# Feature attention of a perceiver block on one core: both sides held transposed, scores on 32 rows, the norm in the exponent, the division on 128x128

## What is computed

```python
def favorplus_features(x, proj):
    xw = jnp.einsum('bhtd,hmd->bhtm', x, proj)
    xw = xw - jnp.max(xw, axis=-1, keepdims=True)
    x_norm_sq = jnp.sum(x * x, axis=-1, keepdims=True)
    return jnp.exp(xw) * jnp.exp(-0.5 * x_norm_sq) + EPS
...
Q = heads(Wq) / math.sqrt(dk)
K = heads(Wk) / math.sqrt(dk)
V = heads(Wv)
phiQ = favorplus_features(Q, proj) * inv_sqrt_m
phiK = favorplus_features(K, proj) * inv_sqrt_m
KV = jnp.einsum('bhtm,bhtd->bhmd', phiK, V)
Ksum = jnp.sum(phiK, axis=2)
num = jnp.einsum('bhtm,bhmd->bhtd', phiQ, KV)
den = jnp.einsum('bhtm,bhm->bht', phiQ, Ksum)[..., None] + EPS
out_heads = num / den
return jnp.einsum('btd,ed->bte', merged, Wo) + bo
```

## Time and profile before

| | us |
|---|---|
| median of 3 runs | 4464.28 |
| runs | 4464.1 to 4465.34 |
| the profiled execution, its own time | 4462.0 |
| its span, first to last instruction | 4460.2 |
| TensorE busy, of the span | 4198.4 (94%) |
| VectorE busy | 2030.8 (46%) |
| ScalarE busy | 1409.1 (32%) |
| GpSimd busy | 159.6 (4%) |
| mean granted clock of TensorE | 0.970 |

### The profile page before, as it was taken

One profiled execution on the slowest core, in us unless ns is written; L12 is line 12 of the kernel. 1 busy time (PEld: TensorE's weight loads), 2 busy tenths in 40 slices (PEclk: granted clock), 3 DMA queues, 4 the chain that ended last, 5 costly groups with the idle time before them and its releaser, 6 DMA issues. The chain is left out here.

```text
span 4460.2 us, 60595 instructions
## 1 busy us (share of the span) xinstructions
PE 4198.4 (94%) x24096; PEld 2764.1 (62%) x24096; DVE 2030.8 (46%) x4307; ACT 1409.1 (32%) x3812; POOL 159.6 (4%) x167
## 2 busy tenths in 40 slices
PE   8999999999999998998799989999999999986885
PEld 4767676767677666665464435666666666763443
DVE  3333333333333333255443334666666666564445
ACT  3222222222222321344231003444444444332232
POOL 0000000000000000022110000000000000000000
PEclk9999999999999999999899999999999999997887
DMA  4010101010101001201304002111011011001000
GB/s 161 29 48 29 54 22 57 25 52 29 57 20 57 29 19 52 96 20 39 99 20 137 0 27 77 44 51 42 25 52 42 24 53 48 1 1 43 0 0 26
DMA packets 86512, 190.47 MB, mean 43 GB/s; under 512 B 7792, under 2 KB 16624, under 8 KB 84464
## 3 DMA queue, kind: packets, MB, share of 16 engines
q1 hardware_dynamic: 73072, 138.60, 9.3%
q0 software_dynamic: 13184, 48.24, 3.4%
HBM read 170.04 MB, written 16.78 MB: 42 GB/s over the span
## 5 line engine op out<-in xcount | busy, mean ns | idle before, releaser
L470 PE MATMUL swishmax_attended<-swishmax_weights_t,swishmax_context 128*128 128x256 f32 x4096 | 905.1, 379 | 0.0
L470 PEld LDWEIGHTS swishmax_attended<-swishmax_weights_t,swishmax_context 128*128 128x128 f32 x4096 | 768.4, 190 | 99.2
L1393 PE MATMUL context_bank<-context_context_t,context_wk 128*128 128x512 f32 x1024 | 475.6, 607 | 17.6 <-DMA context_context_t<-in_context_t_dram 17.6
L485 PE MATMUL swishmax_bank<-swishmax_context_t,swishmax_w_key 128*128 128x512 f32 x1024 | 476.1, 608 | 15.1 <-DMA swishmax_context_t<-in_context_t_dram 15.1
L1262 ACT ACTIVATE context_exps<-context_score,context_neg_max 128x512 f32<-128x512 f32 x512 | 345.1, 686 | 379.6 <-DVE context_neg_max L1296 379.6
L352 ACT ACTIVATE swishmax_xes<-swishmax_score,swishmax_neg_max 128x512 f32<-128x512 f32 x256 | 164.4, 687 | 839.2 <-DVE swishmax_neg_max L389 839.2
L1393 PEld LDWEIGHTS context_bank<-context_context_t,context_wk 128*128 128x128 f32 x1024 | 185.0, 190 | 298.8 <-issue 292.0
L1296 DVE TENSOR_REDUCE context_neg_max<-context_score 128x1 f32<-128x512 f32 x512 | 317.5, 682 | 113.4 <-PE context_score L1361 113.3
L485 PEld LDWEIGHTS swishmax_bank<-swishmax_context_t,swishmax_w_key 128*128 128x128 f32 x1024 | 185.2, 190 | 296.6 <-issue 295.1
L389 DVE TENSOR_REDUCE swishmax_neg_max<-swishmax_score 128x1 f32<-128x512 f32 x256 | 164.7, 685 | 426.8 <-PE swishmax_score L456 426.8
L1408 PEld LDWEIGHTS context_bank<-whole_ident,context_exps 128*128 128x128 f32 x2048 | 229.1, 141 | 119.2 <-issue 69.7
(11 more groups left out here) (341 smaller groups left out, 4838.1 us busy)
## 6 DMA issues: line engine op xcount, KB each, us to landing
swishmax_context_t<-in_context_t_dram SPq DMA_DIRECT2D x32, 1024.0 KB, 5.3
swishmax_context<-in_context_dram POOLq DMA_DIRECT2D x32, 1024.0 KB, 5.8
context_context_t<-in_context_t_dram SPq DMA_DIRECT2D x32, 1024.0 KB, 5.4
ahead_context_t<-in_context_t_dram SPq DMA_DIRECT2D x14, 1024.0 KB, 6.5
ahead_values<-ahead_staged SPq DMA_DIRECT2D x14, 1024.0 KB, 8.4
context_values<-ahead_values POOLq DMA_DIRECT2D x56, 256.0 KB, 3.5
experts_w<-in_L_ffn_W_dram SPq DMA_DIRECT2D x16, 512.0 KB, 8.5
whole_x<-in_x_dram SPq DMA_DIRECT2D x8, 256.0 KB, 8.1
```

What stands on the lines that cost most here:

```text
L470: last = nc.tensor.matmul(attended[m // 2][:, m % 2, :], context[:, c, k, m * P:(m + 1) * P], weights_t[:, n % 2, k].rearrange("p r q -> p ...
L485: last = nc.tensor.matmul(bank_t[:], w_key[:, k, g * P:(g + 1) * P], context_t[:, c, k, :], start=k == 0, stop=k == DC - 1)
L1393: last = nc.tensor.matmul(bank_t[:], w["k"][:, k, g * P:(g + 1) * P], context_t[:, c, k, :], start=k == 0, stop=k == DC - 1)
```

## The change

`kernel_attention` is written anew; its inputs, and the other parts, stay, but for two counters in them that become one (`first = link = Chain(dve, chain)`).

- The sides are made transposed at once: the weights are the stationary operand and the normed tokens the moving one, 16 matmuls of 128 columns each; `side`, side_t and their transposes go.
- Scores are 16 matmuls of 32 rows by 128 columns a side, each head on its own quarter of the array's rows; score bank r holds head r of each group. `proj` is no longer block-diagonal: four loads, no zeros.
- The norm: ScalarE squares the transposed side, TensorE sums it per head with a matrix of ones of four columns (norms, 8 matmuls for both sides), VectorE writes -norm/2 + log(1/sqrt(m)), adds it to the negated maximum, and the exponential takes that as its bias. ScalarE writes the features; EPS is added by VectorE on the query side and by GpSimd on the key side, 128x512 at a time.
- `values` has 64 columns a head: 32 values, and 32 of which column h//4 is one. From the sums, den (one 128x128 for all heads, 16 matmuls on 32 columns of the array each, accumulated) and num (likewise, 128x512) come out transposed. VectorE adds EPS to the 128x128 and inverts it; a matmul with `select` spreads each row over its head's 32 rows; VectorE multiplies. heads_t needs no transposes.
- The loop over pairs is gone. In slot t the engines make the front of sequence t, the scores of t-1 and the back of t-2, by three lists, one for each engine, over ten slots. One ring of four banks serves both emptying engines.
- The output bias is added to x ahead of time, by GpSimd. The first sequence no longer waits for `loaded`.

The diff, cut to its core, the removed lines left out (they stand above):

```diff
...
+        hidden_t = s.sb("hidden_t", [P, 2, DC, P])
+        side_t = s.sb("side_t", [P, 2, 2, NG, P])
+        squares_t = s.sb("squares_t", [P, 2, 2, NG, P])
+        half_norm = s.sb("half_norm", [P, 2, 2, HG, NG])
+        values = s.sb("values", [P, 2, H, 2 * HD])
+        neg_max, exp_bias = s.sb("neg_max", [P, 2, 2, HG, NG]), s.sb("exp_bias", [P, 2, 2, HG, NG])
+        features = s.sb("features", [P, 2, 2, HG, NG, M])
+        features_t = s.sb("features_t", [P, 2, HG, NG, P])
+        sums = s.sb("sums", [P, 2, H, 2 * HD])
+        select = s.sb("select", [P, NG, P])
+        number = s.sb("number", [P, NG, P])
+        inverse = s.sb("inverse", [P, P])
+        heads_t = s.sb("heads_t", [P, NG, P])
...
+        bank = [s.ps(f"bank{n}", [P, CH]) for n in range(4)]
+        score = [s.ps(f"score{r}", [P, CH]) for r in range(HG)]
...
+        def pe_slot(t):
+            p, c, o = t < B, 0 <= t - 1 < B, 0 <= t - 2
+            out = [("score", t - 1, KEY)] * c + [("features_t", t - 2, r) for r in range(HG)] * o + [("hidden", t, 0)] * p
+            out += [("den", t - 2, 0)] * o + [("side", t, QUERY)] * p + [("num", t - 2, 0)] * o
+            out += [("score", t - 1, QUERY)] * c + [("side", t, KEY)] * p + [("spread", t - 2, 0)] * o + [("value", t, 0)] * p
+            out += [("norms", t, QUERY), ("norms", t, KEY)] * p + [("output", t - 2, 0)] * o
+            return out + [("sums", t - 1, 0), ("sums", t - 1, 1)] * c
...
+        def dve_slot(t):
+            p, c, o = t < B, 0 <= t - 1 < B, 0 <= t - 2
+            out = [("max", t - 1, KEY, 0)] * c + [("features_t", t - 2, 1), ("features_t", t - 2, 3)] * o
+            out += [("max", t - 1, KEY, r) for r in (1, 2, 3)] * c + [("den", t - 2, 0)] * o
+            out += [("side", t, QUERY)] * p + [("norm", t + 1)] * (t + 1 < B)
+            out += [("max", t - 1, QUERY, r) for r in range(HG)] * c + [("side", t, KEY)] * p
+            out += [("heads", t - 2)] * o + [("norms", t, QUERY), ("norms", t, KEY)] * p
+            out += [("feature", t - 1, QUERY, r) for r in (0, 1)] * c + [("output", t - 2, 0)] * o
+            return out + [("feature", t - 1, QUERY, r) for r in (2, 3)] * c + [("sums", t - 1, 0)] * c
...
+        pe_steps = [x for t in range(B + 2) for x in pe_slot(t)]
+        act_steps = [x for t in range(B + 2) for x in act_slot(t)]
+        dve_steps = [("norm", 0)] + [x for t in range(B + 2) for x in dve_slot(t)]
+        BY_SCALAR = {("value", 0), ("features_t", 0), ("features_t", 2), ("hidden", 0), ("num", 0), ("sums", 1)}
+        ring = SharedRing(bank, [t for t in pe_steps if t[0] != "score"], {"a": full_a, "d": full_d}, {"a": out_a, "d": out_d},
+                          lambda t: "a" if (t[0], t[2]) in BY_SCALAR else "d")
...
+                pool.wait_ge(loaded, 16 * LOADS)
+                for b in range(B):
+                    pool.wait_ge(normed_x, b + 1)
+                    nc.gpsimd.tensor_tensor(x_sb[:, b, :], x_sb[:, b, :], bias_o[:], ALU.add).then_inc(biased_x, 1)
+                    for r in range(HG):
+                        pool.wait_ge(exped, set_no(b, KEY) * HG + r + 1)
+                        nc.gpsimd.tensor_scalar(features[:, b % 2, KEY, r], features[:, b % 2, KEY, r], EPS * INV_SQRT_M, None,
+                                                ALU.add).then_inc(key_featured, 1)
...
+                    if what == "exp":
+                        r = t[3]
+                        act.wait_ge(biased, set_no(b, n) * HG + r + 1)
+                        for g in range(NG):
+                            last = nc.scalar.activation(features[:, e, n, r, g, :], score[r][:, g * M:(g + 1) * M], ACT.Exp,
+                                                        bias=exp_bias[:, e, n, r, g:g + 1])
+                        last.then_inc(exped, 1)
+                    elif what == "square":
+                        act.wait_ge(out_d, ring.count(("side", b, n)))
+                        nc.scalar.activation(squares_t[:, e, n], side_t[:, e, n], ACT.Square).then_inc(squared, 1)
...
+                    if what == "max":
+                        q, r = t[2], t[3]
+                        if r == 0:
+                            dve.wait_ge(out_d, ring.count(("norms", b, q)))
+                        dve.wait_ge(scored, set_no(b, q) * HG + r + 1)
+                        link(nc.vector.tensor_reduce(neg_max[:, e, q, r, :], score[r][:].rearrange("p (g m) -> p g m", m=M),
+                                                     AX.X, ALU.max, negate=True))
+                        nc.vector.tensor_tensor(exp_bias[:, e, q, r, :], neg_max[:, e, q, r, :], half_norm[:, e, q, r, :],
+                                                ALU.add).then_inc(biased, 1)
...
+                    if what == "heads":
+                        t = ("spread", b, 0)
+                        dve.wait_ge(out_a, ring.count(("num", b, 0)))
+                        dve.wait_ge(full_d, ring.count(t))
+                        nc.vector.tensor_tensor(heads_t[:], number[:], ring.bank(t)[:].rearrange("p (g q) -> p g q", q=P), ALU.mult).then_inc(out_d, 1)
+                        continue
+                    n = t[2]
+                    dve.wait_ge(full_d, ring.count(t))
+                    bank_t = ring.bank(t)
+                    if what == "den":
+                        nc.vector.tensor_scalar(inverse[:], bank_t[:, 0:P], EPS, None, ALU.add).then_inc(out_d, 1)
+                        dve.wait_ge(out_d, ring.count(t))
+                        nc.vector.reciprocal(inverse[:], inverse[:]).then_inc(inverted, 1)
...
+                    if what == "score":
+                        k = set_no(b, n)
+                        evicted(("side", b, n))
+                        pe.wait_ge(loaded, 16 * LOADS)
+                        if k:
+                            pe.wait_ge(exped, k * HG)
+                        for g in range(NG):
+                            for r in range(HG):
+                                rows = slice(r * HD, (r + 1) * HD)
+                                last = nc.tensor.matmul(score[r][:, g * M:(g + 1) * M], side_t[rows, e, n, g, :], proj[rows, g, :],
+                                                        start=True, stop=True)
+                                if g == NG - 1:
+                                    last.then_inc(scored, 1)
+                        continue
...
+                    elif what == "side":
+                        evicted(("hidden", b, 0))
+                        name = "qk"[n]
...
+                                last = nc.tensor.matmul(bank_t[:, g * P:(g + 1) * P], w[name][:, c, g * P:(g + 1) * P], hidden_t[:, e, c, :],
+                                                        start=c == 0, stop=c == DC - 1)
...
+                    elif what == "norms":
+                        pe.wait_ge(squared, 2 * b + n + 1)
+                        pe.wait_ge(grouped, 1 + HG)
+                        for g in range(NG):
+                            last = nc.tensor.matmul(bank_t[:, g * HG:(g + 1) * HG], squares_t[:, e, n, g, :], group[:], start=True, stop=True)
...
+                        for g in range(NG):
+                            for r in range(HG):
+                                last = nc.tensor.matmul(bank_t[r * HD:(r + 1) * HD, 0:P], sums[:, e, HG * g + r, HD:2 * HD],
+                                                        features_t[:, e, r, g, :], start=g == 0, stop=g == NG - 1)
+                    elif what == "num":
+                        for g in range(NG):
+                            for r in range(HG):
+                                last = nc.tensor.matmul(bank_t[r * HD:(r + 1) * HD, g * P:(g + 1) * P], sums[:, e, HG * g + r, 0:HD],
+                                                        features_t[:, e, r, g, :], start=True, stop=True)
+                    elif what == "spread":
+                        pe.wait_ge(inverted, b + 1)
+                        pe.wait_ge(selected, NG)
+                        for g in range(NG):
+                            last = nc.tensor.matmul(bank_t[:, g * P:(g + 1) * P], select[:, g, :], inverse[:], start=True, stop=True)
...
```

346 lines of the change are left out of this document (132 added, 214 removed).

## The result

The changed kernel takes 4335.51 us (median of four runs, 4330.9 to 4336.68), the kernel before 4464.19 in the same comparison: a ratio of 0.9711, 95% interval 0.9694 to 0.9727. It is 129 us faster, as forecast (4335.5). The profiled execution took 4336.0 us, 2.0 more than its span.

What follows compares the result with a forecast made beforehand. The stage was taken as bound by TensorE's own work, its unoverlapped waits and the clock falling for both; slot work, waits and clock summed to 244.1 us, 128.8 off the end, so 4335.5 us, range 4320 to 4368.

Steps and rivals of the forecast that it cites:

- The sum: Whole attention stage, all ten slots: 244.1 us from 4023.91, its end 128.8 us earlier, median 4335.5 us.
- TensorE's work, 26.6 and 0.3 for tiling: One full slot: 26.6 us of TensorE matmuls, plus some 0.3 lost between whole-array and 32-row or 32-column ones.
- The wait at den: In a full slot, TensorE idle 0.95 us ahead of den until ScalarE empties the third features_t bank.
- an excursion: In a slot, switching from whole-array to 32-row or 32-column matmuls and back: four a slot, some 0.3 us together.
- eight changes at the 0.2 of the prediction: Tiling-mode switches in a slot, by the skill's drain rule: no more than 0.2 us each, total 13 us later.
- Slots 0 to 2 and the tail: Stage's ends: slot 0 18.4 us, slot 1 21.1, slot 2 27.9; last two 21.3 and 11.9, plus 4 for clock.
- The start: Head of the stage: the 9.27 us wait for `proj` goes, 9.3 us of the gain.
- A fall in nearly every slot: Rival, chance 0.20: clock falls in every slot, 3.5 us each, seven of them 24.5, giving 4360 us.
- tiles don't overlap: Rival, chance 0.04: scores, den and num cost 0.228 a matmul, 83 us more, giving 4419 us.
- The stretch at 4000: Context part's last stretch: clock stays 1.00 over 9 us, transposes 1.97 us of every 3.2; evidence against the clock falling.
- half clock throughout: Rival, chance 0.02: low-column work keeps the clock at half for the whole stage, 205 us more, 4541 us.
- no change: Rival, chance 0.01: the emptying engines bound the stage after all; a slot would have to be 44 us.

Runs made afterwards that it cites:

- the fourth kernel: The changed kernel with TensorE's hidden transposes ahead of the feature transposes, ScalarE copying them first, and den behind the Q side: 4320.75 us, ratio 0.9684.
- the fifth experiment: The change's instructions, none added or left out, ordered one sequence after the other without overlap: 4435.46 us, ratio 0.9944.
- experiment 1: The changed kernel with the output projection moved ahead of the norms, so that norms and sums are neighbours: 4351.0 us, ratio 0.9746.
- experiment 10: The changed kernel with each of a slot's 16 feature transposes issued twice: 4347.34 us, 11.8 more than the change.
- experiment 9: Kernel with hidden transposes first and a shorter tail (4316.17 us), with the output projection moved ahead of the norms: 4325.44 us.
- experiments 11: The changed kernel with ScalarE copying the hidden transposes ahead of the first exponentials in slots 0 and 1 alone: 4329.64 us.
- experiment 6: The kernel before the change, with VectorE's wait for the loads moved to its first use of the bias: 4462.31 us, ratio 0.9996.
- experiment 2: The changed kernel with the score loops exchanged, so four matmuls in a row use the same 32 rows: 4358.31 us, ratio 0.9764.

## Why the prediction was right

**The sum.** Forecast 244.1 us for the stage, measured 242.9; the last part 63.5 as before (63.4). With the start at 4027.60 instead of 4023.91 that is 4336.0 for the profiled execution against 4333.2 forecast; the median agrees to 0.1 us, which is luck within runs that spread over 6.

**TensorE's work, 26.6 and 0.3 for tiling.** Measured 27.23 in a slot, from start to start. Scores 2.21 (2.2), den and num 1.01 each (1.02), spread 0.89 (0.91), norms 1.70 (1.75), and the sides 7.44 (7.3) were right to 0.15. The sums were not: 3.61 for 3.42, as 64 columns cost 0.226 a matmul, like 128 and not like 33. The feature transposes (1.80 for 1.72) and the output (3.52 for 3.43) were 0.1 dearer each. Together 0.3 a slot too low.

**The wait at den.** Forecast 0.95, measured 0.65. So the slot came out at 27.9 by two errors of 0.3 that cancel, which is luck too; the place of the wait and its releaser, ScalarE's copy, were right. In the fourth kernel den takes 0.90 with num directly behind it, in the change 1.01 with the Q side behind it, so 0.1 for an excursion; the slot's whole excess over the row prices is 0.6. The Trainium skill (TensorEngine Tiling, Key Properties) says that changing the tiling mode drains TensorE. The trace agrees in kind and not in size: eight changes at the 0.2 of the prediction would have been 1.6 a slot.

**Slots 0 to 2 and the tail.** Slot 0 17.3 for 18.4. Slot 1 24.6 for 21.1, slot 2 29.3 for 27.9: the step that failed is slot 1 as work plus waiting, at full clock. I priced its 2.14 us idle (as 2.6), and no fall of the clock, where the rows above have two: 5.39 for 3.84 us at the Q side, 5.50 for 3.68 at the sums. The two last slots took 32.4 us for 37.2: 20.6 and 11.7 where I had 33.2 and 4 more for the clock; the clock fell once, at 4246.7, and cost about 1.5 us, and slot 8 waited 5.0 us for the 7.3 forecast. So 4.9 too few in slots 1 and 2 and 4.8 too many at the end: the clock was right in sum (about 9 us for 8) and wrong in place, so that the stage came out to 1.2 us is luck as well. The 128x128 reciprocal took 0.95 us (1.1), GpSimd's addition 1.49, just over its bound of 1.41, and hidden.

**Where the gain came from.** The forecast said 34 of work, 9.3 of start, 50 of clock, the rest idle time. Work: 8 times 30.9 less 27.2 is 30. The clock's cost in the stage went from 4 times 12.6 to about 9 us: 41. The start is the term that the runs do not bear out as written: in the kernel before, its removal alone gave nothing measurable, and in the change it is worth 4 to 6.5. The remainder, some 50, is idle time inside the turns. And by the fifth experiment the parts are not to be added: cheaper operations in a serial order gave 27 of the 130, since there the waits take 9.2 us of each sequence and the half clock 5.8.

**The rivals.** A fall in nearly every slot is real (five of six in experiment 1) and was avoided by the order; one fall a slot costs 15.5 us (experiment 1, 4351) where the rival had 24.5 (4360), as a fall took 3.1 and not 3.5 and five slots had one, not seven. That tiles don't overlap gives 4358 and not 4419: only the scores were tried, and their serial price was 0.172. In experiment 10 the clock stayed at 1.00 over 147 us, with 4.0 us of transposes together in every slot. The Trainium skill (TensorE: Matmul & The Clock Gate, Part 4) says that transposes do not count as busy in the same way. That is not borne out here: the rival of experiment 10, which made them count as idle time, had a fall in each of these slots. The stretch at 4000 says the same less strongly than the prediction has it: transposes are 4.6 of its 9 us, so 1.97 of every 4.0 and not of every 3.2. The two other rivals, half clock throughout and no change, are excluded by the windows.

## What to carry to other kernels

When one engine is the bound and is late only because others hand it work, look first at the order: sequences offset by a slot, one list for each engine, made the same instructions 103 us faster. Where few-column matmuls can't be avoided, put a wide one between them, and put what the next projection needs at the head of the other engine's list: in slot 1 that took away 1.05 us of waiting and, where the clock stayed up, 4.3 us of time. And do not price an idle stretch by its own length alone: give it a chance of half clock over the work behind it, both when it is removed and when it is added.

## What was not expected of the hardware

- The clock falls with TensorE fully busy: 3.1 us a slot by the order of two groups alone, in five slots of six (experiment 1), and in two of six with no idle time at all (experiment 9). The same order comes out both ways (sums of 6.26 and of 3.77 us in slot 1, experiments 11 and 4). A study of such a change needs several runs and the windows' clock, as one profile can be the one with the fall.
- The old kernel's 9 us of waiting, taken away, gained nothing measurable (0.9996); in the profiled execution the same instructions behind the next wait took 53.29 for 46.97 us, at a lower clock (experiment 6).
- 32-row matmuls take 0.069 us each when neighbours use different rows and banks and 0.172 when they use the same (experiment 2); the loop order alone is 1.65 us in each 16.
